# Slot one's FFN units moved behind slot two's, in a kernel of eight attention and FFN slots on one core

## The reference

```
xn = layernorm(x)                       # over the 2048 columns
t = Wt @ c;  p = Wp @ xn;  g = Wg @ c   # 512x512 weights
att[group] = sum(p * g)                 # 8 groups of 64 channels
y = blockdiag(Wz) @ (att * t)           # Wz: 8 blocks of 64x64
x1 = x + c + groupnorm(y) * gn_w + gn_b # per group, over 64 x 2048
h = layernorm(x1)[:, perm]              # 16 heads of 128 columns
h = gelu(h @ up[head]) @ down[head]     # 128 -> 512 -> 128
out = x1 + unpermute(h)
```

## Time and profile before

| | us |
|---|---|
| median of 3 runs | 1622.25 |
| lowest and highest | 1620.82, 1624.69 |
| the profiled execution | 1625.33 |
| its span, first to last instruction | 1623.5 |
| TensorE busy | 1531.8 (94%) |
| VectorE busy | 1289.8 (79%) |
| ScalarE busy | 975.0 (60%) |
| GpSimd busy | 887.0 (55%) |
| HBM traffic, mean | 230 GB/s |

### The profile page before, as it was taken

How to read it: one execution, slowest core, us unless ns; L and a number is a source line. 1 busy time by engine, 2 the same in 40 slices (tenths; PEclk the granted TensorE clock), 3 DMA queues, 4 the chain that set the end, 5 groups by cost and what they waited for, 6 DMA issues and landing times.

```text
span 1623.5 us, 19290 instructions
## 1 busy us (share of the span) xinstructions
PE 1531.8 (94%) x6592; PEld 1232.5 (76%) x6592; DVE 1289.8 (79%) x1736; ACT 975.0 (60%) x1061; POOL 887.0 (55%) x765
## 2 busy tenths in 40 slices
PE   8988898999999999999989999999999999987997
PEld 7877676877778887788767887777877788765885
DVE  5977979795996879779797788968799687965664
ACT  4325447734787357763667537774377734885885
POOL 1384437156981258613685237941389223975885
PEclk9999999999999999999999999999999999999999
DMA  8888958685685837667385764848559484569785
GB/s 320 292 285 336 306 196 306 230 290 203 229 312 166 252 124 254 243 219 227 116 273 219 226 206 157 301 171 246 162 184 328 116 267 155 164 175 275 235 288 179
DMA packets 126289, 374.77 MB, mean 231 GB/s; under 512 B 24561, under 2 KB 32753, under 8 KB 118001
## 3 DMA queue, kind: packets, MB, share of 16 engines
q1 hardware_dynamic: 91888, 251.88, 47.2%
q0 software_dynamic: 34304, 121.66, 22.0%
HBM read 287.45 MB, written 86.03 MB: 230 GB/s over the span
## 4 chain that ended last, share of the span: by engine, by line
PE 42%; DVE 17%; POOL 15%; DMA 11%; issue 8%; ACT 4%; SPq 2%; POOLq 0%; DVEq 0%; ACTq 0%
PE PP L848 12%; PE PP L834 10%; PE PP L902 8%; PE PP L887 8%; POOL FB L1254 5%; PE PP L861 5%; POOL FB L1251 4%; POOL FB L1239 3%; DVE X L1028 2%; DVE R L1016 2%; POOL out L1259 2%; DMA FB<-xg_scratch,perm_sb 2%; DMA X<-in_x 2%; DVE Z L1133 2%; DVE R L1022 2%
## 5 line engine op out<-in xcount | busy, mean ns | idle before, releaser
L887 PE MATMUL PP<-GG,WW 128*128 128x512 f32 x1536 | 399.4, 396 | 43.0 <-issue 16.1
L887 PEld LDWEIGHTS PP<-GG,WW 128*128 128x128 f32 x1536 | 283.9, 189 | 128.3 <-issue 67.8
L834 PE MATMUL PP<-R 128*128 128x512 f32 x1536 | 360.7, 394 | 18.8 <-DVE R L1016 17.2
L848 PE MATMUL PP<-R,WC 128*128 128x512 f32 x1536 | 354.9, 392 | 7.8 <-ACT Z L933 4.4
L834 PEld LDWEIGHTS PP<-R 128*128 128x128 f32 x1536 | 291.1, 190 | 83.7 <-issue 16.0
L848 PEld LDWEIGHTS PP<-R,WC 128*128 128x128 f32 x1536 | 289.9, 189 | 71.6 <-ACT Z L933 8.0
L979 ACT ACTIVATE R<-PP 128x1024 fp32r<-128x1024 f32 x175 | 179.9, 1028 | 165.5 <-PE PP L887 163.9
L902 PE MATMUL PP<-R,WW 128*128 128x512 f32 x1050 | 269.6, 392 | 6.7 <-DVE R L1168 5.3
L980 ACT ACTIVATE PP<-PP 128x1024 f32<-128x1024 f32 x256 | 261.7, 1022 | 0.0
L1016 DVE TENSOR_TENSOR R<-RAW,R 128x1024 fp32r<-128x1024 f32 x128 | 169.8, 1331 | 85.7 <-ACT R L921 85.2
L902 PEld LDWEIGHTS PP<-R,WW 128*128 128x128 f32 x1050 | 195.1, 188 | 51.2 <-issue 10.7
(11 more groups left out here) (91 smaller groups left out, 1644.5 us busy)
## 6 DMA issues: line engine op xcount, KB each, us to landing
WW<-w_scratch SPq DMA_DIRECT2D x152, 512.0 KB
X<-in_x SPq DMA_DIRECT2D x32, 1024.0 KB, 5.8
RAW<-in_cx SPq DMA_DIRECT2D x32, 1024.0 KB
RAW<-in_xT SPq DMA_DIRECT2D x63, 512.0 KB
RAW<-in_cT SPq DMA_DIRECT2D x63, 512.0 KB
xg_scratch<-FB POOLq DMA_DIRECT2D x104, 256.0 KB, 6.2
w_scratch<-WW POOLq DMA_DIRECT2D x16, 1024.0 KB, 5.8
RAW<-in_Wg SPq DMA_DIRECT2D x8, 1024.0 KB
```

Source lines behind the costliest of these rows:

```text
L834: t = eng.matmul(s_bank(c1), l[:, part(c1)], r, start=(dt == 0 and j == 0), stop=(dt == ND - 1 and j == 2))
L848: t = eng.matmul(PP[2 + ot // 2][:, ot % 2, :], WC[:, l, ct, part(ot)], u[:, r + ct, :], start=(ct == 0 and j == 0), stop=(ct == NT - 1 an ...
L887: t = eng.matmul(PP[slot["up", f, p]][:, e, :], wt[:, l, part(2 * p + e)], g[:, r, :], start=(j == 0), stop=(j == 2))
```

## The change

Slot one has no FFN units any more; slot two runs its 16 units and then the eight of batch 0 (heads 8 to 15), so its FFN has 24. The base of slot two goes from step 88 to 72, and slot three's stays at 156. The times of slot two's s loads, splits, statistics, context additions, x1 pieces and x loads, and the halves of R it uses, are now those of slot one; slot one takes the close spacing of x1 pieces and squares of slot zero. All sixteen heads' weights are split one every five steps from step 16 to step 95, over slots zero to two, through FB[0..3]. The turns of slots zero and one all go through SMM, at 3.3 steps apart. `s_fix`, `s_evh` and `s_evl` stand 0.6 steps later in slots zero to two. `spread_sd` of slots zero and one stands in slot two. The bank of the group statistics and the place of Wp's low part follow.

```diff
--- before.py
+++ after.py
@@ -24,26 +24,26 @@
 EPS = 1e-5
 NRAW = 3
 NFB = 6
-TURN = [(15.9, 19.0, 22.3, 25.5)] + [(10.2, 15.0, 19.6, 24.2)] * 6
+TURN = [(15.9, 19.2, 22.5, 25.8)] * 2 + [(10.2, 15.0, 19.6, 24.2)] * 5
 SBT = 5
 UPS = (0, 2, 3)
 S_EARLY = ([(-1 + 0.2 * dt, 0.5 + 0.2 * dt) for dt in range(4)],
            [(2.0, 2.5), (2.25, 2.75), (3.0, 3.25), (3.5, 3.75)])
 S_LOAD = (-13, -10, -7, -2.8, -1, 3.2, 4.8, 6.8)
-S_FIRST = ((-5.9, -4.9, -3.9, -2.9), (-9.9, -7.9, -5.9, -3.9))
+S_FIRST = (-9.9, -7.9, -5.9, -3.9)
 S_LATE = {4: 2.55, 5: 2.8, 6: 3.3, 7: 4.4}
 
 
 def units(i):
 
-    if i == 0:
+    if i < 2:
         return []
-    if i == 1:
-        return [(h, [0]) for h in range(8, 16)]
     half = [8 * (i % 2) + h for h in range(8)]
     if i == 2:
         half = half[6:] + half[:6]
     ws = [(h, [i - 2, i - 1]) for h in half]
+    if i == 2:
+        ws += [(h, [0]) for h in range(8, 16)]
     if i == B - 1:
         rest = [8 * ((i + 1) % 2) + h for h in range(8)]
         ws += [(h, [i - 1]) for h in rest[:6]] + [(h, [i - 1, i]) for h in rest[6:]]
@@ -100,10 +100,10 @@
 
     def parts(i):
 
-        return (1, 2) if i == 0 or i % 2 else (2, 1)
+        return (1, 2) if i == 1 or i % 2 == 0 else (2, 1)
 
     def s_half(i, dt):
-        k = (dt + 2 * (i == 1)) % 4
+        k = (dt + 2 * (0 < i < 3)) % 4
         return ("R", 0 if k < 2 else parts(i)[0], k % 2)
 
     def y_unit(i, q):
@@ -249,7 +249,7 @@
         order.append(("load_wpl", i))
 
     def load_wg(i):
-        k = slot["wg", i] = slot["c", i, 3] if i == 2 else ring("raw", NRAW)
+        k = slot["wg", i] = ring("raw", NRAW)
         free["wg", i] = take(("raw", k))
         n.dma("wg", i, sem=f"raw{k}")
         order.append(("load_wg", i))
@@ -273,7 +273,7 @@
         order.append(("v_att", i, ot))
 
     def g_bank(i):
-        return (3, 1) if i == 0 else (1, 1)
+        return (3, 1) if i < 2 else (1, 1)
 
     def g_mean_mm(i):
         free["gm", i] = take(("PP", *g_bank(i)))
@@ -372,7 +372,7 @@
         if ct == 0:
             if i < B - 1:
                 fb, sm = [("FB", k) for k in range(4)], [("SM", k) for k in range(2)]
-                slot["tb", i, q] = sm if i == 0 and q % 2 else fb
+                slot["tb", i, q] = sm if i < 2 else fb
             else:
                 slot["tb", i, q] = [("raw", ring("raw", NRAW))]
             free["tb", i, q] = take(*slot["tb", i, q])
@@ -388,16 +388,13 @@
 
     def raw_w(h):
 
-        if 4 <= h < 8:
-            return [("raw", slot["c", 2, 1 + h // 2 % 2])]
-        k = 2 * (h % 2) if h > 7 else 4
+        k = 2 * (h % 2)
         return [("FB", k), ("FB", k + 1)]
 
     def load_raw(h):
-        sem = f"rh{h}" if 4 <= h < 8 else f"rw{h % 2 if h > 7 else 2}"
         free["rw", h] = take(*raw_w(h))
-        n.dma("rw", h, sem=sem, count=2)
-        slot["rw", h] = raw_w(h)[0], sem
+        n.dma("rw", h, sem=f"rw{h % 2}", count=2)
+        slot["rw", h] = raw_w(h)[0], f"rw{h % 2}"
         order.append(("load_raw", h))
 
     def w_hi(h):
@@ -544,20 +541,15 @@
     for pr in range(2):
         put(10.5 + 0.1 * pr, fold_hi, pr)
         put(10.7 + 0.1 * pr, fold_lo, pr)
-    for k in range(8):
-        t = 15 + 2.6 * k
-        put(t, load_raw, 8 + k)
-        put(t + 4, w_hi, 8 + k)
-        put(t + 4.1, w_lo, 8 + k)
-        put(t + 4.2, keep_w, 8 + k)
-    for h in range(4):
-        t = 38 + 4 * h
+    for k in range(ND):
+        t = 16 + 5 * k
+        h = (8 + k) % ND
         put(t, load_raw, h)
-        put(t + 2.6, w_hi, h)
-        put(t + 2.7, w_lo, h)
-        put(t + 2.8, keep_w, h)
-
-    base = [0, 36, 88] + [88 + 68 * k for k in range(1, B - 2)]
+        put(t + 4, w_hi, h)
+        put(t + 4.1, w_lo, h)
+        put(t + 4.2, keep_w, h)
+
+    base = [0, 36, 72] + [88 + 68 * k for k in range(1, B - 2)]
     f = 0
     w = 0
     w_used = {}
@@ -565,34 +557,29 @@
     for i in range(B):
         s0 = base[i]
         y0, v0, f0 = s0 + 16, s0 + 32, s0 + 36
-        first = i == 0
-        for k, h in enumerate((4, 5, 6, 7) if i == 2 else ()):
-            put(y0 + (2.5, 5.2)[k // 2], load_raw, h)
-            put(y0 + 5.6 + 1.8 * k, w_hi, h)
-            put(y0 + 5.7 + 1.8 * k, w_lo, h)
-            put(y0 + 5.8 + 1.8 * k, keep_w, h)
+        first = i < 2
         for j in range(8):
-            put(s0 + (S_LOAD[j] if i > 1 else 0.3 if (i, j) == (1, 2) else 2 * j - (5 if i or j else 10)), load_s, i, j)
+            put(s0 + (S_LOAD[j] if i > 2 else 0.3 if i and j == 2 else 2 * j - (5 if i or j else 10)), load_s, i, j)
         for dt in range(ND):
-            t = s0 + (dt - 2.6 if i < 2 else S_FIRST[i > 2][dt] if dt < 4 else S_LATE.get(dt, dt - 2.6))
+            t = s0 + (dt - 2.6 if i < 3 else S_FIRST[dt] if dt < 4 else S_LATE.get(dt, dt - 2.6))
             put(t, s_hi, i, dt)
             put(t + 0.2, s_lo, i, dt)
             for c1 in range(NT):
-                put(s0 + (dt + 0.25 * c1 if i < 2 or dt > 3 else S_EARLY[c1 // 2][dt][c1 % 2]), s_mm, i, dt, c1)
+                put(s0 + (dt + 0.25 * c1 if i < 3 or dt > 3 else S_EARLY[c1 // 2][dt][c1 % 2]), s_mm, i, dt, c1)
         for q in range(NQ):
             for ct in range(NT):
-                t = s0 + 2.2 + 3.3 * ct + 0.8 * q if i == 2 else s0 + (4 * q + ct) * 0.85 + 0.9
-                t = 10.4 + 1.4 * ct + 0.22 * q if first else s0 + 9.3 + 1.6 * ct + 0.4 * q if i == 1 else t
+                t = s0 + (4 * q + ct) * 0.85 + 0.9
+                t = 10.4 + 1.4 * ct + 0.22 * q if i == 0 else s0 + 9.3 + 1.6 * ct + 0.4 * q if i < 3 else t
                 put(t, bn_x, i, ct, q)
-        if first:
+        if i == 0:
             for ct in range(NT):
                 put(5.4 + 1.7 * ct, load_x, i, ct)
         put(y0 + 2, aggr_x, i)
         put(y0 + 2.1, root_x, i)
-        late = 1.0 if i == 1 else 0
+        late = 1.0 if 0 < i < 3 else 0
         for q, t in enumerate((s0 + 9, s0 + 11, s0 + 13, y0 + 1.5 + late)):
             put(t, load_c, i, q)
-        put(y0 + (9 if i == 2 else 2.5 + late), load_wg, i)
+        put(y0 + 2.5 + late, load_wg, i)
         for q, t in enumerate((y0 - 3, y0 + 0.4, y0 + 4.3, y0 + 8.3)):
             put(t, y_hi, i, q)
             put(t + 0.2, y_lo, i, q)
@@ -603,9 +590,9 @@
         put(y0 + 5.9 + late, store_sum, i)
         put(y0 + 7.6 + late, spread_sum, i)
         for c1 in range(NT):
-            put(y0 + 11.3 + 0.6 * c1, s_fix, i, c1)
-            put(y0 + 11.5 + 0.6 * c1, s_evh, i, c1)
-            put(y0 + 12.2 + 0.6 * c1, s_evl, i, c1)
+            put(y0 + 11.3 + (0.6 if i < 3 else 0) + 0.6 * c1, s_fix, i, c1)
+            put(y0 + 11.5 + (0.6 if i < 3 else 0) + 0.6 * c1, s_evh, i, c1)
+            put(y0 + 12.2 + (0.6 if i < 3 else 0) + 0.6 * c1, s_evl, i, c1)
         for q in range(NQ):
             for ot in range(NT):
                 put(y0 + 4 * q + ot, y_mm, i, q, ot)
@@ -618,8 +605,8 @@
             put(y0 + 1, load_wph, i)
             put(y0 + 12.1, load_wpl, i)
         for ot in range(NT):
-            put(v0 + ot + (0.5 if i and ot == NT - 1 else 0), v_mm, i, ot)
-            put(v0 + ot + (1.4 if i and ot == NT - 1 else 0.95), v_att, i, ot)
+            put(v0 + ot + (0.5 if i > 1 and ot == NT - 1 else 0), v_mm, i, ot)
+            put(v0 + ot + (1.4 if i > 1 and ot == NT - 1 else 0.95), v_att, i, ot)
         put(v0 + 3.4, aggr_y, i)
         put(f0 + 1.2, g_mean_mm, i)
         put(f0 + 1.25, g_mean, i)
@@ -632,18 +619,18 @@
         last = i == B - 1
         for k in range(8):
             ct, hf = k // 2, k % 2
-            t = f0 + 5 + 0.8 * k if first else f0 + 7.25 + (1.2 if i == 1 else 1.33 if last else 2) * k
+            t = f0 + 5 + 0.8 * k if first else f0 + 7.25 + (1.33 if last else 2) * k
             put(t, x1_piece, i, ct, hf)
             put(t + (0.9 if first else 1.2) if first or last else base[i + 1] + 0.9 + 0.55 * k, square_x1, i, ct, hf)
             if hf and not last:
-                put(base[2] - 1.5 + 3.3 * ct if i == 1 else t + 0.1, load_x, i + 1, ct)
+                put(t + 0.1, load_x, i + 1, ct)
         put(f0 + (4.1 if first else 5.26), mean_x1, i)
         e = f0 + 12 if first else f0 + 18.4 if last else base[i + 1] + 5.4
         put(e, sum_sq, i)
         put(e + 0.1, root_x1, i)
         put(e + 0.9, shift_x1, i)
         put(e + 1.2, store_sd, i)
-        put(f0 + 30 if last else f0 + 29.5 if i == 0 else e + 5, spread_sd, i)
+        put(f0 + 30 if last else base[2] + 29.5 + 0.1 * i if first else e + 5, spread_sd, i)
         for ct in range(NT):
             put(e + 1.1 + (0.6 if first else 1.8 if last else 0.9) * ct, xln2, i, ct)
         for q in range(NQ):
@@ -790,10 +777,10 @@
         return R[k[0]][:, 4 * k[1] + 2 * lo:4 * k[1] + 2 * lo + 2, :]
 
     def wpl_unit(i):
-        return R[2 if i % 2 else 1] if i else GG
+        return R[1 if i > 2 and i % 2 else 2] if i else GG
 
     def g_bank(i):
-        return PP[3][:, 1, :] if i == 0 else PP[1][:, 1, :]
```

(1 more changed line is left out.)

## The result

| | before | after |
|---|---|---|
| median of 4 runs, us | 1622.42 | 1645.41 |
| lowest and highest | 1620.82, 1624.69 | 1644.06, 1648.21 |
| profiled execution, its span | 1625.33, 1623.5 | 1644.06, 1642.2 |

The ratio after to before is 1.0134, 95% interval 1.0116 to 1.0151. The change costs 23.0 us by the medians and 18.7 us between the two profiled executions. The forecast was +10.9 and 1633 us: right in sign, half the size. The time lies inside the whole range (1612 to 1648), near its upper end, and outside the likeliest case's own (1626 to 1641).

The account below looks back on a forecast made before the run. TensorE bounds the kernel (1480 of 1623.5 us its own), so only idle time moves. Terms -4 + 4 + 13.7 + 4 - 6.8 give +10.9, 1633 us against the 1622.25 median; range 1612 to 1648, likeliest case 1626 to 1641.

Parts of the forecast that it names:

- Part 5: Turns of slots zero and one through one buffer: each waits for the last store's landing; +4 us each in slots one, two.
- (5.1 us): Median landing time of SMM stores, cited for the rival in which the single turn buffer's wait is hidden.
- Part 1: Slot two's attention becomes a copy of slot one's, priced by slot one's measured row, 123.12 against 109.42 us: +13.7.
- Part 2: Slot one's eight FFN units move to slot two's end: 45 us in, 47.75 and 4.08 out, -6.8.
- Parts 3 and 4: Later s_fix, s_evh, s_evl and spread-out weight splits together: -4 us in slot zero, bounds 0 and -4.4.
- part 3: s_fix, s_evh, s_evl 0.6 later in slots zero to two, so y_ev(2,1) goes first and 4.1 us leave that place.
- part 4: Head splits spread to about 14 us apart; less weight traffic before slot zero's sum_c, which ends some 3 us earlier.
- The rule on the shared port: GpSimd splits in y stages of slots one and two each hold VectorE 2 to 3 us; sum some 4 us higher, 1637.
- A: Rival: VectorE reaches each turn after or nearly after the landing, so the single buffer costs nothing; -5.6 us, 1617, chance 0.19.
- C: Rival: gains and losses cancel, slot two's s stage losing half and turns costing 3 us; 1622 to 1625, chance 0.13.
- B: Rival: a w_hi waiting on POOL holds store_x and the next turn; another +5 in slots one, two; 1643 to 1650, chance 0.18.

Follow-up runs that it names:

- e3: Changed kernel with w_hi and w_lo of all heads but 8 and 9 cut to 8 of 512 columns, transfers kept: 1632.1 us, ratio 1.0031 to the kernel before.
- e2: Changed kernel with turn 1 of slots zero and one moved behind y_lo(2) and add_c(2) in VectorE's order: 1647.94 us, ratio 1.0136 to the kernel before.
- e1: Changed kernel with turns of slots zero and one through two buffers again, raw weights and bny placed elsewhere: 1619.46 us, ratio 0.9968 to the kernel before.
- e11: Kernel before with only the last two s loads of slot one issued ahead of load_x: 1623.11 us, ratio 0.9982.
- e4: Changed kernel with s_fix, s_evh and s_evl back at their old times in slots zero to two: 1648.79 us, ratio 1.0146 to the kernel before.
- e5: Kernel before with only s_fix, s_evh and s_evl 0.6 steps later in slots zero and one: 1623.86 us, ratio 0.999.
- e8: Changed kernel with two turn buffers and weight splits bunched outside the s stages, raw load to w_hi in 2.8 steps: 1655.08 us, ratio 1.017 to the kernel before.
- e10: Changed kernel with load_wg (1 MB) of slots zero to two issued 3.5 to 4.5 steps later: 1651.74 us, ratio 1.0159 to the kernel before.
- e6: Changed kernel with load_wph (1 MB) 6 steps later in slots one and two: 1645.32 us, ratio 1.0119 to the kernel before.

## Why the prediction was right in sign and too small

*Part 5 is the step that failed:* "I take +4 in slot one and +4 in slot two". Held against slot one's row of before, slot one lost 5.6 us and slot two 134.83 - 123.12 = 11.7: 17.3 for 8, a miss of 9.3. The chain that part 5 works through can be held against the changed kernel step by step, in us from the first y matmul:

| | part 5 | slot one | slot two |
|---|---|---|---|
| store 0 issued | 9.6 | 10.2 | 10.2 |
| turn 1 | 17.2 | 21.6 | 22.2 |
| turn 2 | 28.6 | 32.5 | 35.3 |
| turn 3 | 40.3 | 43.9 | 48.1 |
| s_fix(0) | 44.1 | 47.5 | 51.6 |
| Wp stage | 52.1 | 55.8 | 60.0 |

The mechanism was right, and so was the price of the slow clock in the Wp stage (1.7 forecast, 1.7 and 1.9 measured). What was wrong, in order of weight:

- The landing of store 0 was taken as 7.7 us, from the only wait of that kind in the trace of before. It took 11.4 and 12.0 us, and the 3.7 and 4.3 us too much go through the whole chain to the Wp stage. For store 2 the 7.7 was near (7.2 and 8.5). (5.1 us) was further off still: it is a median of single DMAs over all places, while a turn waits for the last of four that GpSimd needs 2.6 us to issue, and the four of store 0 took 7.6 to 9.4 us each.
- The price was made the same for both slots, because slot two's turns are slot one's. In slot two the Wp stage starts 7.9 us later than part 5 has it. Beyond the landing of store 0, some 2.5 us are the add_c held beside a w_lo, ahead of turn 2 (e3's rows), and 0.8 the landing of store 2.
- Against this, the s stages were 2.4 and 0.5 us shorter than slot one's of before, which the forecast did not have.

I had also not asked what else is queued behind turn 1 on VectorE. It is y_lo(2), and TensorE stopped there for 6.83 and 7.42 us. That was overlooked, but it isn't a price of its own: with y_lo(2) first (e2) the same time is lost at the end.

e1 is the evidence for the whole: with the second buffer slot one takes 114.35 us and slot two 117.55, where they took 124.62 and 134.83. That is 27.6 us back, more than the 17.3, because both slots are then shorter than slot one of before (119.04 without its FFN matmuls, 123.12 with them).

*Part 1, +13.7: right, in part by luck.* Slot two's s stage became slot one's, 58.0 us for 58.6. But with the turns in another order (e2) the same s stage took 53.3 us, and with two buffers (e1) 52.1, so that it came out the same is in part chance. And the cause given for such a stage, "what lies between the slots", with load_x in the sync queue ahead of the s loads, is only one of two. e3 shows the splits on GpSimd to cost 7 to 10 us in each s stage. e11 shows the loads to cost 5.6 us of the stage in the kernel before, 4.4 of them given back in the y stage.

*Part 2, -6.8: wrong by 4.1 us.* The 24 units take 139.49 - 90.37 = 49.1 us more than 16 did, for the 45 taken, and 192 matmuls at 0.2268 us are 43.5. Of the 5.6 us between, 4.4 are the two waits for weights. So "the gain of the change", as part 2 calls it, was not there. The -2.7 that the account shows, outside part 2's bounds (-7.8 and -3), are just the twelve s matmuls of slot two that the earlier trace rows has in slot one's FFN window: before, the eight units took 47.75 + 4.08 - 2.72 = 49.1 us as well. In the other traces with this FFN, it takes 135 to 143 us from its first group matmul to slot three's first s matmul, for 136.8 in the changed kernel's. Without the -4.9 of the rest, the miss between the two traces would be 12.7 us and not 7.8.

*Parts 3 and 4, -4 in slot zero: the value right, the reason half.* Measured -4.7, with some 2 us of scatter (slot zero, unchanged, ended at 114.03 in e11 for 115.84). By e4 and e5 the 0.6 steps of part 3 have no share that can be told. What is left is part 4, the weights spread out, which no run tests by itself.

*The rule on the shared port.* The slowing of VectorE beside w_lo, seen once in the earlier trace rows and weighed at 4 us over two y stages, is the larger effect: 8.9 us of VectorE's busy time in one s stage. The Trainium skill ("SBUF — State Buffer", section "SBUF: two separate sides") says that the one of the two engines that starts second is blocked until the first is done. The trace agrees in kind: the s_lo of 3.39 us ends 1.07 us after the w_lo that started before it. The estimate from that rule, 1637, was on the right side of mine and still too low.

*The rivals.* A (single buffer hidden) is refuted by VectorE's waits for the landings and by e1. C did not occur: slot two's s stage lost what slot one's does. B had the time nearly right (1643 to 1650) by a mechanism that was not there: in slots one and two GpSimd waited for VectorE at each of the eight stores, never in a w_hi with a store due. e8 then showed that GpSimd standing at a late load can cost tens of us.

## What to carry to other kernels

When a staging buffer goes from two to one, price the whole cycle (fill, issue, landing under the traffic of that place, next fill) times the number of fills against the stage that holds it, and list what stands behind each fill on its engine. Moving one victim ahead only moves the wait. Take the landing from the place where it will lie: here the first of four stores took about half as long again as the third. When stages of two kernels are compared, let the windows end at the same instruction and check the counts. When side work goes on GpSimd, count VectorE's busy time with and without it for the same instructions, not GpSimd's own. And give in-order side work slack behind its loads, or the small operations behind it will carry the load's latency to all engines.

## What was not expected of the hardware

- The same 52 VectorE instructions took 45.82 us beside GpSimd's full splits (three w_hi and four w_lo) and 36.93 us beside cut ones; a 128x1024 subtraction took 3.39 us and not 1.21.
- A 1 MB store in four DMAs of 256 KB landed 11.4 and 12.0 us after its first issue, and the same store later in the same stage 7.2 and 8.5 us, against a median of 5.1 for a single DMA. Moving a 1 MB load away from it left 12.0 (e10) and 11.4 in one slot and 9.4 in the other (e6). What delays it is open.
- After a wait of 7 us, 96 matmuls take 1.7 to 2.0 us longer than without one (23.71 for 22.02, 24.03 for 22.00), so that such a wait costs a quarter to a third more than it lasts.
